# Index bits of the weight look-up: int32 and-operations on VectorE in place of float comparisons on GpSimd

## The chip, the cores and the metric

The kernel runs on one core of a Trainium2 chip. The core has a matrix engine (TensorE, PE in the rows), a vector engine (VectorE, DVE), an activation engine (ScalarE, ACT), a general engine (GpSimd, POOL) and an engine that issues transfers (SyncE, SP), all working side by side on a memory of 128 partitions (SBUF); matmuls write to PSUM. The metric is the device time of one execution in microseconds, the median of several.

## The reference, cut to what matters

Four layers, each an attention-like block and a feed-forward block, are applied to x (4 x 256 tokens of 256 values). The change touches the weights of the third feed-forward block, which come as 4-bit indices into a table of 16 numbers:

```python
def _ghost_linear(x, idx, lut):
    w = lut[idx]                       # lut: 16 floats, idx: int32 in 0..15
    return jnp.einsum('bsh,oh->bso', x, w)
gate = _ghost_linear(x, gate_idx, lut) # 688 x 256 indices
up = _ghost_linear(x, up_idx, lut)     # 688 x 256
h = jax.nn.silu(gate) * up
return _ghost_linear(h, down_idx, lut) # 256 x 688
```

The look-up itself needs only the indices and the table. The kernel therefore does it ahead, beside the block before: the third attention (16 heads, 4 batches, two softmaxes on one set of queries).

## The kernel before, in words

Each engine has one program, written out by hand, and they meet through semaphores; there is no planner. What stands next on an engine's program waits for what stands before it.

The 4288 index words of each partition lie in `w2` (the tensor `regD`) and are looked up in `LUT_PIECES` = 8 pieces of `LP` = 536 words. With the index written in bits b3 b2 b1 b0, a piece goes so:
- Bits. GpSimd casts the piece to float in `left` (`lut_b0`, two buffers, L611), and three times compares with 8, 4 or 2, times that number (the mask `lut_m`, L613), and subtracts (L614). What remains in `left` is b0 as 0.0 or 1.0. `lut_bits` counts pieces.
- Leaves. ScalarE computes, for each pair of table entries, `lut[2*leaf] + b0 * (lut[2*leaf+1] - lut[2*leaf])` over the piece (L979, `lut_leaves`): 8 leaves of a piece in 4 calls of 2 (`k` = 0 to 3).
- Picks. VectorE's `copy_predicated` chooses between leaves by the masks of 2, 4 and 8 (L1612, `choose` in `lut_step`): 7 picks, counted by `lut_pick`. The result replaces the indices in `w2`.

All of this is threaded through the attention's 64 steps (batch b, head h, i = 16 b + h). Piece p starts at VectorE's step i = `LUT_START` + `LUT_STEPS` * p = 5 + 7 p; its sub-steps 2 to 6 are the picks, and ScalarE has its leaves at sub-steps 1 to 4. GpSimd is not threaded: its loop over the pieces runs on its own, held back only by `lut_pick` of the piece two before, which frees the buffers (and by `q2_mm` for piece 1, whose masks lie in the room of `xnT`).

In a step of the attention, TensorE does the shifted scores of head h (L2218, L2219), some scores of the next batch (L2198), and the values of the head before (L2234); ScalarE takes the exponential (L994); VectorE takes the maxima of the next batch's scores (L1574, L1575), which free the score banks, and every fourth head normalises (L1593 to L1599). At h = 13 VectorE splits the next batch's maxima into three bf16 parts (L1582 to L1585); TensorE transposes them (L2205), ScalarE copies them out (L969), and the next batch's shifted scores need them. In between stand the query projection of the second half (L2066, L1402 and what follows), the splitting of queries (L963 to L1567), the output product (L2083) and its addition (L1420, L1421). The feed-forward block that uses the weights begins near 852 us.

Names of tensors in the rows: `regD` holds the pieces and one `left`, `regC` the other `left` and a leaf, `regB` the masks of even pieces and a leaf, `xnT` the masks of odd pieces, `ctxT` a leaf.

Of the kernel before, what the change touches and what calls it, by code (L numbers as in the profile page):

```python
# [17 lines left out]
I32 = mybir.dt.int32  # L18
U32 = mybir.dt.uint32
ALU = mybir.AluOpType  # L20
ACT = mybir.ActivationFunctionType
# [3 lines left out]
B, S, DIM, CDIM = 4, 256, 256, 128  # L25
# [37 lines left out]
def build(nc, a, out):  # L63
    with ExitStack() as ctx:
        def sb(name, shape, dt=F32):
            return ctx.enter_context(nc.sbuf_tensor(name, shape, dt))

        def sem(name):
            return ctx.enter_context(nc.semaphore(name))
# [31 lines left out]
        def carve(region):  # L101
            at = [0]

            def take(*shape, dt=F32):
# [9 lines left out]
                if len(shape) > 1:  # L114
# [138 lines left out]
        w2 = regD[:, 0:2 * NG + ND]  # L253
# [3 lines left out]
        LUT_PIECES = 2 * B  # L257
        LP = (2 * NG + ND) // LUT_PIECES
# [7 lines left out]
        lut_b0 = [w2_room, lut_b0]  # L266
        lut_m = [[tB(LP) for _ in range(3)], xnT_room]
        lut = sb("lut", [P, LUT])
        lutd = sb("lutd", [P, LUT // 2])
# [31 lines left out]
        ld_raw, ld_1, ld_f1, ld_2, ld_i2, ld_3, ld_f3 = (  # L301
            sem(n) for n in ("ld_raw", "ld_1", "ld_f1", "ld_2", "ld_i2", "ld_3", "ld_f3"))
# [9 lines left out]
        stk_f, stk_h, stk_r, stk_m, stk_done, stk_tr, stk_out, shift_set, v2_set = (  # L312
            sem(n) for n in ("stk_f", "stk_h", "stk_r", "stk_m", "stk_done", "stk_tr", "stk_out", "shift_set", "v2_set"))
        q2_mm, q2_out, s2_mm, max2, mxs_done, mx_tr, mxT_done, st_mm, exp2, o2_mm, o2_norm, co_tr, coT_done, wo2_mm, wo2_add = (
            sem(n) for n in ("q2_mm", "q2_out", "s2_mm", "max2", "mxs_done", "mx_tr", "mxT_done", "st_mm", "exp2", "o2_mm",
                             "o2_norm", "co_tr", "coT_done", "wo2_mm", "wo2_add"))
        lut_bits, lut_leaf, lut_pick, sx_done, z_done, z_tr, z_add, bf_done, hw_mm, wd3_done, hs3_done, xh_mm, xh_out = (
            sem(n) for n in ("lut_bits", "lut_leaf", "lut_pick", "sx_done", "z_done", "z_tr", "z_add", "bf_done", "hw_mm", "wd3_done",
                             "hs3_done", "xh_mm", "xh_out"))
        stored = sem("stored")  # L320

# [115 lines left out]
        def _(pool):  # L437
            chain = [0]

            def link(ins, base=0):  # L440

                chain[0] += 1
                ins.then_inc(plc, 1)
                pool.wait_ge(plc, base + chain[0])
# [76 lines left out]
            with pool.Fori(1, H0 // 2 - 1) as hp:  # L521
                for par in range(2):
                    n = hp * 2 + (par - 2)
# [76 lines left out]
                    pool.tensor_tensor(shiftw, shift0[:, 0:H2].unsqueeze(2).to_broadcast([STK, H2, S]),  # L600
                                       shift0[:, H2:].unsqueeze(1).to_broadcast([STK, H2, S]), ALU.mult).then_inc(shift_set, 1)

            pool.wait_ge(ld_i2, 16 * 5)
            pool.wait_ge(stk_out, 4 * B)
            for i in range(LUT_PIECES):
                left = lut_b0[i % 2]
                if i == 1:
                    pool.wait_ge(q2_mm, 4)
                if i >= 2:
                    pool.wait_ge(lut_pick, 7 * (i - 1))  # L610
                link(pool.tensor_copy(left, w2[:, i * LP:(i + 1) * LP].bitcast(I32)))  # L611
                for m, bit in zip(lut_m[i % 2][::-1], (8.0, 4.0, 2.0)):
                    link(pool.tensor_scalar(m, left, bit, bit, ALU.is_ge, ALU.mult))  # L613
                    ins = pool.tensor_tensor(left, left, m, ALU.subtract)  # L614
                    if bit > 2:
                        link(ins)
                ins.then_inc(lut_bits, 1)
            for n in range(10, 12):
                ln_pow(n)

# [1 line left out]
            for st in range(3):  # L622
                step = 1 << st
                src = bf[st % 2].rearrange("p (g two s) n -> p g two s n", two=2, s=step)
                dst = bf[(st + 1) % 2].rearrange("p (g two s) n -> p g two s n", two=2, s=step)
# [11 lines left out]
        def _(act):  # L637
# [186 lines left out]
            for b in range(B):  # L824
                act.wait_ge(nb1_done, b + 1)
                for q in range(2):
                    act.activation(p1[b][:, q, :], bank(b)[:, q * S:(q + 1) * S], ACT.Exp,
                                   bias=nb1[:, b, q:q + 1], accum_out=ls1[:, b, q:q + 1]).then_inc(exp1, 1)
# [15 lines left out]
            for tt in range(NT):  # L844
                for nb in range(2):
                    i = 2 * tt + nb
# [4 lines left out]
                if tt < B:  # L851
                    act.wait_ge(rl1_done, tt + 1)
                    for q in range(2):
                        last = act.activation(p1[tt][:, q, :], p1[tt][:, q, :], ACT.Copy, scale=ls1[:, tt, q:q + 1])
# [116 lines left out]
            def lut_leaves(i, k):  # L971

                act.wait_ge(lut_bits, i + 1)
                used = 7 * i + (0, 0, 1, 3)[k]
                if used:
                    act.wait_ge(lut_pick, used)
                to = (w2[:, i * LP:(i + 1) * LP], lutC, lutD, lutC)[k]
                for dst, leaf in ((to, 2 * k), (lut_alt[k % 2], 2 * k + 1)):
                    last = act.activation(dst, lut_b0[i % 2], ACT.Identity, scale=lutd[:, leaf:leaf + 1], bias=lut[:, 2 * leaf:2 * leaf + 1])  # L979
                last.then_inc(lut_leaf, 1)  # L980

            act.wait_ge(df_mm, 2 * TPH)
# [5 lines left out]
            for b in range(B):  # L988
                for h in range(H2):
                    i = b * H2 + h  # L990
                    act.wait_ge(st_mm, i + 1)
                    if i >= 3:
                        act.wait_ge(o2_mm, i - 2)
                    act.activation(pT2[i % 3].rearrange("p k q -> p (k q)"), bank(4 + i % 2), ACT.Exp,  # L994
                                   scale=float(HD2) ** -0.5).then_inc(exp2, 1)
                    if h in STACK2 and b + 1 < B:
                        stack_out(B + b + 1, STACK2.index(h))
                    if b == 0 and h == LNT9:
                        ln_out(9)
                    if b == 0 and h == QNORM + 2:  # L1000
                        deviations(B + 1, TPH)
                    if b + 2 < B and h == SPLIT2[b]:
                        stack_parts(b + 2)
                    if h == COT2 and b:
                        heads_out2(b - 1)
                    if h == SHIFT2 and b + 1 < B:
                        maxima_out(b + 1)
                    piece, step = divmod(i - LUT_START, LUT_STEPS)
                    if 0 <= piece < LUT_PIECES and 1 <= step < 5:
                        lut_leaves(piece, step - 1)  # L1010
# [8 lines left out]
        def _(dve):  # L1019
# [586 lines left out]
            def lut_step(i, step):  # L1606

                A = w2[:, i * LP:(i + 1) * LP]
                m1, m2, m3 = (m.bitcast(U32) for m in lut_m[i % 2])

                def choose(to, m, other):
                    dve.copy_predicated(to, m, other).then_inc(lut_pick, 1)  # L1612

                n = 7 * i
                if 2 <= step <= 5:
                    k = step - 2
                    if k == 0:
                        dve.wait_ge(lut_bits, i + 1)
                    dve.wait_ge(lut_leaf, 4 * i + k + 1)
                    choose((A, lutC, lutD, lutC)[k], m1, lut_alt[k % 2])  # L1620
                    if k % 2:
                        dve.wait_ge(lut_pick, n + (2, 5)[k // 2])
                        choose((A, lutD)[k // 2], m2, lutC)
                elif step == 6:
                    dve.wait_ge(lut_pick, n + 6)
                    choose(A, m3, lutD)

# [5 lines left out]
            for b in range(B):  # L1633
                for h in range(H2):
                    i = b * H2 + h
                    if b + 1 < B:
                        for hn in first_pass(b, h):
                            maxima(b + 1, hn)
                        if h == SHIFT2 - 1:
                            maxima_parts(b + 1)  # L1640
                    if b == 0 and h == LN9:
                        dve.wait_ge(df_add, TPH * 2)
                        layer_norm(9)
                    if b == 0 and 0 <= h - QNORM < 3:
                        queries(1, h - QNORM)
                    piece, step = divmod(i - LUT_START, LUT_STEPS)
                    if 0 <= piece < LUT_PIECES:
                        lut_step(piece, step)
                    if b + 2 < B and h == SPLIT2[b]:
                        stack_rest(b + 2)  # L1650
                    if h % HPB == 2 and i >= HPB:
                        normalise((i // HPB - 1) // HPB, (i // HPB - 1) % HPB)
                    if h == WO2 and b:
                        output2(b - 1)
                    if b == B - 1 and h == WO2 + 2:
                        dve.wait_ge(wo2_add, 2)
                        layer_norm(10)
# [719 lines left out]
```

## Time and profile before

| | us |
|---|---|
| median of 3 runs | 1029.34 (1029.27 to 1031.43) |
| the profiled execution | 1028.96 |
| its span, first to last instruction | 1027.4 |
| PE busy | 867.6 |
| DVE busy | 708.8 |
| ACT busy | 535.8 |
| POOL busy | 448.0 |
| mean granted clock of PE | 0.92 of full |

Times in the rows are microseconds from the span's start unless they are marked ns. A line such as L1612 is a line of the kernel's text. In "out<-in" the tensor written stands first, then those read, then partitions x elements and the type. "idle" is the time that the engine stood before an instruction, and the name behind the arrow is what ended it. An engine's idle time costs nothing unless the engine is on the path to the end, so the rows are to be read as a question: what is late at this point, and for whom.

### The profile page before, as it was taken

What the parts mean: (1) busy time and instruction counts of PE and PEld (TensorE: products, weight loads), DVE (VectorE), ACT (ScalarE), POOL (GpSimd) and SP (SyncE); (2) the same over time, 40 slices, a digit from 0 to 9 for tenths busy, and PEclk for the clock granted to TensorE, in tenths of its full rate; (3) what the DMA queues carried; (4) which work ended last, traced back from release to release, by engine and by line L of the source; (5) the groups of instructions that cost most, each with busy time, mean ns of one, the idle gap of its engine ahead of it and who ended that gap; (6) DMA issues with size and microseconds to landing.
All of it is one profiled execution on the core that took longest, in us unless ns stands there. A gap on an engine that the chain in (4) does not pass through costs nothing.

```text
span 1027.4 us, 13071 instructions
## 1 busy us (share of the span) xinstructions
PE 867.6 (84%) x4348; PEld 615.1 (60%) x4352; DVE 708.8 (69%) x1367; ACT 535.8 (52%) x991; POOL 448.0 (44%) x274
## 2 busy tenths in 40 slices
PE   5795899999999999645579986858688799999998
PEld 3354777777877777513354643728577685545646
DVE  4247689999899998778848566765989863353311
ACT  2486687787778778733313442535678472112120
POOL 1211678777778886556810002007458540600000
PEclk8898899999999999866879998958699899999999
DMA  4003000100000100000520000000000001100000
GB/s 126 16 5 133 16 17 16 31 15 15 15 15 15 31 3 6 1 0 1 198 83 0 1 1 1 1 0 1 2 1 2 1 1 48 83 0 1 12 9 21
DMA packets 12924, 24.25 MB, mean 24 GB/s; under 512 B 4280, under 2 KB 8656, under 8 KB 11728
## 3 DMA queue, kind: packets, MB, share of 16 engines
q1 hardware_dynamic: 12448, 20.53, 6.2%
q10 hardware_dynamic: 432, 3.15, 0.8%
q8 instruction: 26, 0.43, 0.2%
q14 instruction: 18, 0.15, 0.0%
HBM read 22.63 MB, written 1.05 MB: 23 GB/s over the span
## 4 chain that ended last, share of the span: by engine, by line
PE 30%; DVE 14%; issue 4%; ACT 4%; POOL 1%; ACTq 0%; DVEq 0%
PE PS L2131 12%; PE PS L2180 6%; PE PS L2234 3%; DVE mxf L1574 2%; DVE regD L1612 1%; PE PS L2035 1%; PE PS L1674 1%; DVE regB L1612 1%; PE PS L2011 1%; PE PS L2198 1%; PE PS L2049 1%; PE PS L2218 1%; PE PS L2219 1%; DVE xn L1051 1%; PE PS L2083 1%
## 5 line engine op out<-in xcount | busy, mean ns | idle before, releaser
L487 POOL TENSOR_TENSOR X<-X,xn 128x512 f32<-128x512 f32 x62 | 103.4, 1668 | 69.1 <-ACT xn L712 68.6
L454 POOL TENSOR_SCALAR veps<-mv 128x4 f32<-128x4 f32 x16 | 3.6, 228 | 265.9 <-DVE mv L1042 265.8
L1141 DVE TENSOR_TENSOR_SCAN regB<-regB 128x1024 f32<-128x1024 f32 x32 | 85.5, 2671 | 0.2
L1122 DVE TENSOR_SCALAR_CACHE_REDUCE regA<-PS,nrq 128x256 bf16<-128x256 f32 x128 | 56.0, 475 | 38.2 <-PE PS L1749 36.3
L731 ACT ACTIVATE regA<-PS,nb,rq 128x256 f32<-128x256 f32 x128 | 72.1, 576 | 11.7 <-DVE regA L1122 10.9
L2234 PE MATMUL PS<-regA 128*128 128x128 f32 x512 | 74.8, 293 | 3.4 <-ACT regA L994 3.3
L480 POOL TENSOR_TENSOR y<-y,regB 128x1024 f32<-128x1024 f32 x32 | 75.7, 2364 | 3.5 <-DVE regB L1152 3.4
L1771 PE MATMUL PS<-regA 128*128 128x256 f32 x256 | 67.0, 384 | 7.3 <-DVE qss L1109 7.2
L2234 PEld LDWEIGHTS PS<-regA 128*128 128x128 f32 x512 | 68.2, 206 | 7.1 <-ACT regA L994 6.1
L1749 PE MATMUL PS<-regA 128*128 128x256 f32 x256 | 67.1, 385 | 0.0
L1780 PE MATMUL PS<-regA 128*128 128x256 f32 x256 | 66.5, 383 | 0.0
L1722 PE MATMUL PS<-xnT,regA 128*128 128x512 f32 x128 | 60.3, 614 | 4.6 <-ACT regA L702 3.4
L2131 PE MATMUL PS<-xnT,regB 128*128 128x512 f32 x128 | 61.2, 628 | 1.3 <-ACT xnT L642 1.3
L2180 PE MATMUL PS<-regB 128*128 128x256 f32 x256 | 58.8, 388 | 3.6 <-DVE X L1551 3.5
L933 ACT ACTIVATE regB<-PS 128x512 f32<-128x512 f32 (+1 forms) x28 | 16.7, 596 | 84.2 <-PE PS L2131 84.0
L2131 PE MATMUL PS<-regA,regB 128*128 128x512 f32 x128 | 55.8, 594 | 1.4 <-ACT regA L923 1.4
L2180 PEld LDWEIGHTS PS<-regB 128*128 128x128 f32 x256 | 49.2, 194 | 12.6 <-DVE X L1551 4.3
L1771 PEld LDWEIGHTS PS<-regA 128*128 128x128 f32 x256 | 47.3, 192 | 14.2 <-DVE qss L1109 8.4
L1749 PEld LDWEIGHTS PS<-regA 128*128 128x128 f32 x256 | 46.0, 193 | 15.4 <-issue 10.1
L737 ACT COPY regA<-PS 128x512 f32<-128x512 f32 x64 | 38.1, 596 | 29.8 <-PE PS L1760 29.6
L1780 PEld LDWEIGHTS PS<-regA 128*128 128x128 f32 x256 | 49.2, 192 | 6.9
L712 ACT ACTIVATE xn<-PS,ls 128x256 f32<-128x256 f32 x124 | 52.8, 491 | 0.2 <-issue 0.2
(276 smaller groups left out, 2162.6 us busy)
## 6 DMA issues: line engine op xcount, KB each, us to landing
regA<-in_W SPq DMA_DIRECT2D x16, 384.0 KB, 3.0
regB<-in_wg SPq DMA_DIRECT2D x2, 1024.0 KB, 6.5
regB<-in_wu SPq DMA_DIRECT2D x2, 1024.0 KB, 8.5
X<-in_x SPq DMA_DIRECT2D x1, 1024.0 KB, 8.2
regC<-in_wg ACTq DMA_DIRECT2D x1, 1024.0 KB, 5.8
regC<-in_wu ACTq DMA_DIRECT2D x1, 1024.0 KB, 8.0
regC<-in_wd ACTq DMA_DIRECT2D x1, 1024.0 KB, 10.0
regB<-in_wd SPq DMA_DIRECT2D x1, 1024.0 KB, 9.9
```

Of the source, the lines that this page charges most:

```text
L480: pool.tensor_tensor(halves(y3, i), halves(y3, i), halves(prod, i), ALU.add).then_inc(y_done, 1)
L487: pool.tensor_tensor(xt, xt, part, ALU.add).then_inc(x0_add, 1)
L731: act.activation(p0[i][:, q, :], bank(S_BANK + i)[:, q * S:(q + 1) * S], ACT.Exp, bias=nb0[:, i, q:q + 1], scale=rq[par][:, 2 * b + q:2 * ...
L1122: ins = dve.tensor_scalar(spill[:, i, q, :], bank(S_BANK + i)[:, q * S:(q + 1) * S], nrq[par][:, t:t + 1], None, ALU.mult, ALU.min, accum_ ...
L1141: dve.tensor_tensor_scan(v(hs), v(dA), v(dBu), 0.0, ALU.mult, ALU.add).then_inc(scan_done, 1)
L1722: last = pe.matmul(to[:, i * HALF:(i + 1) * HALF], w0[par][:, c * P:(c + 1) * P], xnT[:, c, i * HALF:(i + 1) * HALF], start=c == 0, stop=c ...
L1749: last = pe.matmul(bank(S_BANK + b % 2)[:, q * S:(q + 1) * S], qT[par][:, (2 * b + q) * P:(2 * b + q + 1) * P], kT[par][:, b * S:(b + 1) * S],
L1771: last = pe.matmul(bank(O_BANK)[:, 0:S], ctxN[:, 2 * b + k, :], pT0[b % 2][:, k, :], start=k == 0, stop=k == 1)
L1780: last = pe.matmul(bank(W_BANK)[:, q * DIM:(q + 1) * DIM], oT0[b % 2][:, q * P:(q + 1) * P], wvo[par], start=True, stop=True)
L2131: last = pe.matmul(bank(to)[0:rows, :], w[:, k, c * P:c * P + rows], src[:, k, :], start=k == 0, stop=k == KD - 1)
L2180: last = pe.matmul(bank(6 + td % 2)[:, 0:DIM], hT[0:rows, c, t * P:(t + 1) * P], wd[0:rows, c, :], start=c == 0, stop=c == nch - 1)
L2234: last = pe.matmul(bank(6 + g % 2)[:, at:at + P], pT2[i % 3][:, k, q * P:(q + 1) * P], V2flat[:, v:v + P], start=k == 0, stop=k == 1)
```

## The change

VectorE takes over the bits. At sub-step 0 of a piece (steps 5, 12, 19, 26, 33, 40, 47 and 54) it does four bitwise-ands of the piece as int32: with 2, 4 and 8 for the masks (not zero means choose), and with 1 for b0, which stays an int32 0 or 1. ScalarE reads b0 as int32 and converts it by itself. The loop on GpSimd goes. The waits for the buffers move to VectorE, a new semaphore `lut_mask` counts the masks, and `lut_bits` now comes with the and by 1.

```diff
@@ gpsimd
-            pool.wait_ge(ld_i2, 16 * 5)
-            pool.wait_ge(stk_out, 4 * B)
-            for i in range(LUT_PIECES):
-                left = lut_b0[i % 2]
-                if i == 1:
-                    pool.wait_ge(q2_mm, 4)
-                if i >= 2:
-                    pool.wait_ge(lut_pick, 7 * (i - 1))
-                link(pool.tensor_copy(left, w2[:, i * LP:(i + 1) * LP].bitcast(I32)))
-                for m, bit in zip(lut_m[i % 2][::-1], (8.0, 4.0, 2.0)):
-                    link(pool.tensor_scalar(m, left, bit, bit, ALU.is_ge, ALU.mult))
-                    ins = pool.tensor_tensor(left, left, m, ALU.subtract)
-                    if bit > 2:
-                        link(ins)
-                ins.then_inc(lut_bits, 1)
@@ scalar, lut_leaves
-                    last = act.activation(dst, lut_b0[i % 2], ACT.Identity, scale=lutd[:, leaf:leaf + 1], bias=lut[:, 2 * leaf:2 * leaf + 1])
+                    last = act.activation(dst, lut_b0[i % 2].bitcast(I32), ACT.Identity, scale=lutd[:, leaf:leaf + 1], bias=lut[:, 2 * leaf:2 * leaf + 1])
@@ vector, lut_step
                 A = w2[:, i * LP:(i + 1) * LP]
+                if step == 0:
+                    if i == 1:
+                        dve.wait_ge(q2_mm, 4)
+                    if i >= 2:
+                        dve.wait_ge(lut_pick, 7 * (i - 1))
+                    for m, bit in zip(lut_m[i % 2], (2, 4, 8)):
+                        dve.tensor_scalar(m.bitcast(I32), A.bitcast(I32), bit, None, ALU.bitwise_and).then_inc(lut_mask, 1)
+                    dve.tensor_scalar(lut_b0[i % 2].bitcast(I32), A.bitcast(I32), 1, None, ALU.bitwise_and).then_inc(lut_bits, 1)
...
                     if k == 0:
-                        dve.wait_ge(lut_bits, i + 1)
+                        dve.wait_ge(lut_mask, 3 * i + 3)
```

## Rows read from the trace of the kernel before

**Rows 1.** The page, part 1: busy us, share of the span, instructions.

```profile
PE 867.6 (84%) x4348; PEld 615.1 (60%) x4352; DVE 708.8 (69%) x1367; ACT 535.8 (52%) x991; POOL 448.0 (44%) x274
```

**Rows 2.** Stretches: length, busy us of each engine, PE's granted clock, DMA.

```profile
695.00:742.00 47.00, 35.68 (x243) 30.72 (x241) 34.77 (x70) 25.41 (x35) 27.70 (x19) 0.77 0.00 1
742.00:778.00 36.00, 30.55 (x271) 27.03 (x270) 31.27 (x72) 28.58 (x43) 23.09 (x15) 1.00 0.01 2
778.00:818.00 40.00, 32.24 (x270) 28.56 (x270) 35.19 (x72) 27.06 (x42) 27.77 (x18) 0.96 0.01 2
818.00:852.00 34.00, 31.16 (x243) 27.98 (x243) 25.05 (x55) 22.82 (x38) 12.30 (x9) 0.95 0.00 1
```

**Rows 3.** Chain that ended last, in order of time: start, us, what.

```profile
718.30 1.75 DVE regD L1612
...
739.79 0.88 DVE mxs L1582
...
778.55 1.89 DVE regD L1612
...
808.96 1.61 DVE regD L1612
```

**Rows 4.** Groups of POOL by shape: busy us, mean ns, idle before, releaser.

```profile
L613 POOL TENSOR_SCALAR xnT<-regC 128x536 f32<-128x536 f32 x12 | 26.0, 2168 | 1.1
...
L611 POOL CAST regC<-regD 128x536 f32<-128x536 int32 x4 | 2.5, 629 | 17.0 <-DVE regD L1612 11.8 <-PE PS L2066 5.2
...
L454 POOL TENSOR_SCALAR veps<-mv 128x4 f32<-128x4 f32 x1 | 0.2, 233 | 13.0 <-DVE mv L1042 13.0
```

**Rows 5.** Line 1612: ns min/median/max, first to last start; then its stretch.

```profile
L1612 DVE COPY_PREDICATED regB<-regB,regC x8: 742/758/1805, 723.2 to 832.4; 128x536 f32<-128x536 uint32 x8
...
L1612 DVE COPY_PREDICATED regD<-regB,ctxT x4: 750/752/755, 735.3 to 834.0; 128x536 f32<-128x536 uint32 x4
...
695.00:852.00 157.00, 54.06 (x56) 0.91 0.00 1
```

**Rows 6.** Lines 1574 and 1582: ns min/median/max.

```profile
L1574 DVE TENSOR_REDUCE mxf<-PS x64: 633/652/661, 678.9 to 815.8; 128x2 f32<-128x480 f32 x64
...
L1582 DVE CAST mxs<-mxf x4: 175/402/870, 691.0 to 817.1; 128x64 bf16<-128x64 f32 x4
```

**Rows 7.** Bitwise-ands in the trace, and DVE's timeline at 771 us.

```profile
L1197 DVE TENSOR_SCALAR regA<-regC x6: 672/673/674, 148.4 to 369.5; 128x1024 int32 x6
...
L1192 DVE TENSOR_SCALAR mx_am<-mx_am x6: 181/181/181, 128.0 to 349.0; 128x32 int32<-128x32 int32 x6
...
770.87 0.75 DVE L1612 COPY_PREDICATED regD<-regB,ctxT 128x536 f32<-128x536 uint32 x1
771.52 0.64 DVE L1574 TENSOR_REDUCE mxf<-PS 128x2 f32<-128x480 f32 x1
```

**Rows 8.** DVE's timeline: start, us, instruction, idle before it.

```profile
712.90 0.66 DVE L1574 TENSOR_REDUCE mxf<-PS 128x2 f32<-128x480 f32 x1 [2.79 <-PE PS L2198]
...
788.59 0.66 DVE L1574 TENSOR_REDUCE mxf<-PS 128x2 f32<-128x480 f32 x1 [1.72 <-PE PS L2198]
...
804.47 0.69 DVE L1420 TENSOR_TENSOR X<-X,regC 128x512 f32<-128x512 f32 x1 [1.59 <-PE PS L2083]
...
824.96 0.88 DVE L1612 COPY_PREDICATED regD<-regB,regC 128x536 f32<-128x536 uint32 x1 [3.72 <-ACT regC L979]
```

**Rows 9.** ACT's timeline.

```profile
738.58 0.83 ACT L979 ACTIVATE regD<-regC,lut,lutd 128x536 f32<-128x536 f32 x1
...
742.18 0.37 ACT L969 COPY regB<-PS 96x256 bf16<-96x256 bf16 x1 [1.57 <-PE PS L2205]
...
753.44 0.82 ACT L979 ACTIVATE regD<-regD,lut,lutd 128x536 f32<-128x536 f32 x1
```

**Rows 10.** PE's timeline: the output product twice.

```profile
801.28 3.15 PE L2083 MATMUL PS<-regC,regB 128*128 128x256 f32 x8
...
835.98 1.89 PE L2083 MATMUL PS<-regC,regB 128*128 128x256 f32 x8
```

More of the change, by code:

```diff
@@ L316, in build @@
                              "o2_norm", "co_tr", "coT_done", "wo2_mm", "wo2_add"))
-        lut_bits, lut_leaf, lut_pick, sx_done, z_done, z_tr, z_add, bf_done, hw_mm, wd3_done, hs3_done, xh_mm, xh_out = (
-            sem(n) for n in ("lut_bits", "lut_leaf", "lut_pick", "sx_done", "z_done", "z_tr", "z_add", "bf_done", "hw_mm", "wd3_done",
+        lut_bits, lut_mask, lut_leaf, lut_pick, sx_done, z_done, z_tr, z_add, bf_done, hw_mm, wd3_done, hs3_done, xh_mm, xh_out = (
+            sem(n) for n in ("lut_bits", "lut_mask", "lut_leaf", "lut_pick", "sx_done", "z_done", "z_tr", "z_add", "bf_done", "hw_mm", "wd3_done",
                              "hs3_done", "xh_mm", "xh_out"))
```

## The prediction

> **What bounds the kernel now.** I read the engines' shares first [rows 1]: PE is busy 84% of the span, VectorE (DVE) 69%, GpSimd (POOL) 44%. A mean over stages decides nothing, so next the busy time by stretch around the edited code [rows 2]. The look-up runs beside the 64 steps of the third attention, from 695 to 852 us, and each of the four stretches is about one of its batches. DVE is busy 34.8 of 47 us, then 31.3 of 36, then 35.2 of 40; only in the last batch does it fall to 25.1 of 34, while PE rises to 31.2. So DVE is the fullest engine in the second and third batch, with ScalarE (ACT) close in the second (28.6 of 36). Granted clock is 0.77 in the first stretch and about 1 in the others. The chain of waits says the same [rows 3]: picks (copy_predicated, L1612) and casts of DVE stand on it one after another.
>
> **What is removed.** POOL makes the bits of each piece in one cast (L611), three comparisons (L613) and three subtractions (L614). Per piece that is 0.63 + 3 x 2.16 + 3 x 1.34 = 11.1 us, in all 2.9 + 2.5 + 26.0 + 25.9 + 16.3 + 15.8 = 89.4 us of POOL's 448 ([rows 4] have one line of each buffer). None of it is itself on the path: the last piece's bits were done at 831.9 and its leaves start at 835.3, and the gap is as wide or wider at the others. POOL's next work, the power of a layer norm at 844.88, waited 13.0 us for DVE [rows 4], so it comes no earlier by an empty POOL. Directly the removal is worth 0.
>
> Indirectly it is worth something. A pick takes 742 to 755 ns at its shortest, but up to 1.9 us elsewhere with the same shape; the 56 of them take 54.06 us where 56 x 0.755 = 42.3 would do [rows 5]. Each long one starts or runs while a POOL instruction of a piece is under way; those of 838 us and later, after POOL's last piece, are all 0.76 to 0.77. Casts of 128x64 show it too (870 against 175 ns) and so does one addition by 1.0 us, while the maxima, which read PSUM, stay within 633 to 661 ns [rows 6]. Excess: picks 11.8, casts and remainder-casts 1.7, the addition 1.0, together 14.4 us. By batch it is 2.0, 2.9, 6.9 and 2.6.
>
> The Trainium skill (SBUF — State Buffer, section "SBUF: two separate sides") states that VectorE and GpSimd share one port pair as an exclusive lock, taken for a whole instruction by a VectorE instruction with two SBUF inputs or in a two-port mode, the loser standing still. The trace agrees: picks read two SBUF tensors and stretch by up to 1.1 us, PSUM maxima do not. By that rule the whole 14.4 us goes with POOL's pieces; without it a part could belong to ACT's traffic. It also says that the new operations would stand behind POOL if POOL still ran, which it does not.
>
> **What is added.** 4 bitwise-ands per piece, 32 in all, 128x536 int32. No such shape is in the trace, but its neighbours are: the same operation on 128x1024 takes 673 ns, on 128x32 181 ns [rows 7]. Between them 181 + 504 x 492/992 = 431 ns. Bounds: 181 below; above, 673. I take 0.43, 13.8 us of busy time. On DVE's timeline an instruction without a wait starts 0.10 us before the last one ends (a pick of 0.75 us at 770.87, the next maximum at 771.52 [rows 7]), so four ands push what follows by about 4 x 0.35 = 1.4 us (0.7 to 2.7 with the bounds). No real wait comes with them: q2_mm 4 was already waited for at step 7, the lut_pick counts are DVE's own and a piece old. DVE's total is then 32 x 0.35 = 11.2 us more against 14.4 less. ACT's leaves now read int32 in place of float. No row of ACT has such an input; on DVE the int32 form differs from a float one of the same size by 22 ns (673 to 695), which on 64 leaves is at most 1.4 us either way, half of it where ACT is full. I take 0.
>
> **Where the 1.4 us lands.** The ands stand at steps 5, 12, 19, 26, 33, 40, 47, 54 of DVE's program, and ACT's leaves one step later wait for the last of the four. By pieces:
> - Piece 0 (near 707): DVE then waits 2.79 us before 712.90 [rows 8]. Free.
> - Piece 1 (step 12, behind the maxima ending 739.8): on the chain, +1.4. Ahead of it the pick at 718.30 gives back 1.0, behind it the two casts 1.0 [rows 3]. That leaves -0.6, but ACT, which began its leaves at 738.58, now stands until about 740.2, and the shift copy L969 behind them (742.18) comes no earlier [rows 9]. Sum 0.
> - Piece 2 (step 19, 752.8): DVE 1.0 late at once, ACT's leaves 0.8 late against 753.44 [rows 9]. Picks at 755.6, 758.3 and 759.6 give back 1.2 and DVE's short waits 0.5. At 761.5: -0.5.
> - Piece 3 (step 26, 772.2): DVE has no gap there, +1.4; the cast at 776.5 gives back 0.4, the pick at 778.55 (1.88 us, ACT waits for it) 1.1 [rows 3]. At 780: -0.6.
> - Piece 4 (step 33, 785.8): DVE waits 1.72 us before 788.59 [rows 8]. Free. Then the picks at 789.3, 792.8 and 797.1 give back 2.4 us, but the leaves that they read come from an ACT whose timeline has no gap over 0.35 us from 783 to 796, so I count 1.4 of it. At 801: -2.0.
> - Piece 5 (step 40, 802.8): DVE waits 1.59 us for the output product before 804.47 [rows 8]. Free. Picks at 808.87 and 812.79, both on the chain, the first among the rows [rows 3], give back 0.95 + 0.87. At 818: -3.8.
> - Piece 6 (step 47, 821.2): 3.72 us of waiting before 824.96 [rows 8]. Free. The pick at 826.82 gives back 1.0, of which ACT can use the 0.58 us it waited: -4.4.
> - Piece 7 (step 54, 834.7): DVE has by then 2.5 us more in hand from three shorter picks, ACT's leaves at 835.3 do not wait. Free. From 852 on nothing differs.
>
> Sum -4.4 us. The profiled execution took 1028.96 us, 1027.4 of it span and 1.6 around it; it lies 0.4 under the median of 1029.34. So 1024.6 for a profile like this one and 1024.9 for the median; I say 1025.
>
> **The rivals.** What a measurement here can tell from no change is about 0.2%, 2.1 us.
> - The gain is eaten by ACT and PE. The attention's steps go round DVE, ACT and PE, and ACT is full from 742 to 761 and from 783 to 796. If ACT's pace holds there and again past 806, only the 0.6 of piece 3 and 1 us or so of the 806 to 818 stretch remain: about 1028. For it: ACT 28.6 of 36 us [rows 2]. Against: its waits for DVE's picks in the third batch.
> - Slower. The ands sit in front of ACT's leaves and of the maxima that PE's next scores wait for; at pieces 1, 2 and 3 there is no gap, 3 x 1.4 = 4.2 us, and PE idle there can bring its clock down. The clock's price: the output product of 8 matmuls took 3.15 us at 801.28 after an idle 2 us against 1.89 at 835.98 [rows 10]. With 1.3 to 2.6 for one or two such stretches and a give-back of only 3, it is +3: 1032. It decides if the four ands take more than about 0.5 us a step each, for then piece 4 and 5 outgrow their gaps as well.
> - More than forecast. With DVE ahead, PE does not idle at 799 to 801 and 816 to 818, and the clock stays up: 1.3 (above) and 1 us for the steps at 819 to 822 more. And ACT's caps at 797 fall: 1021.5.
> - The change does not free DVE: the picks stay long without POOL. Then 11.2 us of ands have nothing against them, about half on the path: 1034. The late picks of 0.76 us speak against it, and so does the port rule named above; I give it little.
>
> **How the numbers follow.** Forecast (own range 1022.5 to 1027) 0.52; eaten 0.19; more 0.15; slower by the leaves' wait 0.10; picks stay long 0.04. Faster by over 0.2% (under 1027.3) is the forecast, the larger gain and a sliver of the eaten case: 0.69. Within: most of the eaten case and the mild part of the slower: 0.19. Slower: 0.12. The range takes the larger gain and the eaten case whole and the unknown cost of the ands to its middle: 1020.5 to 1030.5.
>
> **What would show it.** Right: POOL almost empty between 696 and 844; 56 picks at about 42 us, none above 0.8 us; casts near 0.2 us; ands at 0.43 us and 0.35 apart, 13.8 us in all; ACT waiting about 1.6 us for the bits of piece 1 and 0.5 to 1 at pieces 2 and 3, none at 4 to 7; the batches ending 0, 0.6, 3.8 and 4.4 us earlier than 742, 778, 818 and 850. Wrong: ands at 0.6 us or more; picks still of 1 us and over; ACT waiting for bits in the third batch; a clock under 0.9 between 742 and 818; or leaves of over 0.85 us from int32 input.

## The result, and the profile after

The changed kernel takes 1024.55 us (median of 4 runs, 1023.6 to 1025.03) beside 1029.39 for the kernel before: ratio 0.9939 [0.9927, 0.9950]. A second set of runs gave 1024.51 beside 1029.89, 0.9945 [0.9933, 0.9958]. The medians lie 4.8 and 5.4 us apart, and by the ratios it is faster by 6.3 and 5.7 us; 1025.0 was forecast. The profiled execution of after took 1025.03 us, 1023.5 of it span.

The page of the kernel after, part 1, answers to [rows 1]: VectorE is 4.5 us less busy, GpSimd 88.

```profile
PE 867.3 (85%) x4352; PEld 613.2 (60%) x4352; DVE 704.3 (69%) x1399; ACT 535.3 (52%) x991; POOL 360.0 (35%) x218
```

The stretches of [rows 2], after (length, then PE, PEld, DVE, ACT and POOL, granted clock, DMA share, GB/s). Compare the third: PE is busy 36.4 of 40 us where it was 32.2, and the clock is 1.00 in it and in the fourth, where it was 0.96 and 0.95. (The edges of the stretches are fixed, and this execution came to the third attention 2.3 us later than that of before, so a row does not hold quite the same work in both.)

```profile
695.00:742.00 47.00, 36.18 (x252) 31.46 (x252) 34.17 (x78) 25.76 (x35) 1.26 (x2) 0.82 0.00 1
742.00:778.00 36.00, 28.00 (x244) 24.53 (x244) 30.00 (x77) 28.07 (x42) 0.00 (x0) 1.00 0.01 1
778.00:818.00 40.00, 36.41 (x320) 32.53 (x321) 36.55 (x94) 30.23 (x48) 0.00 (x0) 1.00 0.01 2
818.00:852.00 34.00, 30.77 (x234) 26.18 (x232) 22.86 (x59) 23.32 (x37) 1.26 (x2) 1.00 0.00 1
```

DVE's groups by shape in 690 to 850 us of after (busy us, mean ns, idle before). The ands (L1600, L1601) take 431 to 435 ns in the mean of each group, 32 x 0.432 = 13.8 us (the busy column counts their overlaps once). The casts whose median was 402 ns [rows 6] have one of 184.

```profile
L1600 DVE TENSOR_SCALAR xnT<-regD 128x536 int32<-128x536 int32 x12 | 4.5, 433 | 0.0
L1600 DVE TENSOR_SCALAR regB<-regD 128x536 int32<-128x536 int32 x12 | 4.5, 431 | 0.0
...
L1601 DVE TENSOR_SCALAR regC<-regD 128x536 int32<-128x536 int32 x4 | 1.7, 435 | 0.0
L1601 DVE TENSOR_SCALAR regD<-regD 128x536 int32<-128x536 int32 x4 | 1.7, 432 | 0.0
```

The picks, now L1605 (min/median/max ns, first to last start). All 56 lie between 742 and 780 ns; before, the first of these forms went up to 1805 [rows 5].

```profile
L1605 DVE COPY_PREDICATED regB<-regB,regC x8: 742/759/770, 724.6 to 827.4; 128x536 f32<-128x536 uint32 x8
...
L1605 DVE COPY_PREDICATED regD<-regB x4: 754/770/780, 725.3 to 824.3; 128x536 f32<-128x536 uint32 x4
```

The leaves, now L964, from int32 input: as long as from float before ([rows 9] show 0.82 and 0.83).

```profile
L964 ACT ACTIVATE regC<-regD,lut,lutd x16: 817/823/842, 711.4 to 826.5; 128x536 f32<-128x536 int32 x16
```

The chain of waits of after, in order of time (start, us, what). Ands stand on it at pieces 1, 2, 3 and 5, 1.04 + 0.35 us each time, and at no other.

```profile
741.06 1.04 DVE xnT L1600 x3
742.10 0.35 DVE regC L1601
...
755.05 1.04 DVE regB L1600 x3
756.09 0.35 DVE regD L1601
...
774.18 1.04 DVE xnT L1600 x3
775.22 0.35 DVE regC L1601
...
803.38 1.04 DVE xnT L1600 x3
804.42 0.35 DVE regC L1601
```

ACT's timeline in after, the leaves that waited for bits. It stands 2.16 us at piece 1, 0.70 and 0.90 at pieces 2 and 3, and 0.91 at piece 6, where none was expected; 0.25 at piece 0.

```profile
742.49 0.83 ACT L964 ACTIVATE regD<-regC,lut,lutd 128x536 f32<-128x536 int32 x1 [2.16 <-DVE regC L1601]
...
756.47 0.83 ACT L964 ACTIVATE regD<-regD,lut,lutd 128x536 f32<-128x536 int32 x1 [0.70 <-DVE regD L1601]
...
775.60 0.83 ACT L964 ACTIVATE regD<-regC,lut,lutd 128x536 f32<-128x536 int32 x1 [0.90 <-DVE regC L1601]
...
820.01 0.83 ACT L964 ACTIVATE regD<-regD,lut,lutd 128x536 f32<-128x536 int32 x1 [0.91 <-DVE regD L1601]
```

**Where the time went, batch by batch.** One profiled execution enters the third attention earlier or later than another for reasons ahead of it (691.0 to 694.6 us among these traces). So every kernel is measured from its own first cast of the maxima (the mxs cast, L1582 before, L1567 after) to the same cast of each later batch and to the last normalising product. These lengths repeat to 0.1 us between the two traces of the changed kernel. In this table, worked out from DVE's timelines, each column is one batch.

| us | batch 0 | 1 | 2 | 3 | sum |
|---|---|---|---|---|---|
| before | 48.8 | 36.7 | 40.6 | 34.6 | 160.6 |
| after | 49.0 | 37.4 | 34.6 | 33.2 | 154.3 |
| e1, POOL works beside it | 51.3 | 42.9 | 37.7 | 35.1 | 167.0 |
| e2, no ands at pieces 2 to 7 | 49.0 | 35.5 | 34.3 | 32.2 | 151.0 |
| e5, 7 ands a piece | 50.0 | 39.7 | 37.8 | 35.0 | 162.6 |
| e3, pieces 1 to 3 on POOL | 48.8 | 36.7 | 34.6 | 33.2 | 153.2 |
| e4, ands a step earlier | 49.1 | 37.7 | 34.6 | 32.2 | 153.6 |
| e8, pieces 0 and 1 ahead | 47.7 | 36.8 | 35.8 | 33.2 | 153.6 |
| e7, before with matmuls | 48.8 | 36.7 | 39.5 | 32.6 | 157.5 |
| e7 again | 48.8 | 36.7 | 38.3 | 34.6 | 158.3 |
| e10, after with matmuls | 49.0 | 37.4 | 34.6 | 33.2 | 154.2 |
| e9, ahead and POOL | 47.7 | 36.7 | 34.6 | 33.2 | 152.3 |
| e11, that and a step earlier | 47.7 | 36.7 | 34.6 | 32.2 | 151.2 |

The change loses 1.0 us in batches 0 and 1 and gains 6.0 in batch 2 and 1.3 in batch 3: 6.3 in all. What comes before and behind the stage decides how much of that one execution shows. Behind it the traces of before, after and a0_after take 175.8 to 175.9 us each; but after entered the stage 2.3 us later than before did and a0_after 0.9 later, so their profiled executions are only 3.9 and 5.4 us shorter. The stage is the measure of the change, and the total carries this variation with it.

### The profile page after: what moved, and what is told of

It is laid out like the page before. It is cut to its first block, busy times and chain, and to the rows that moved or that the text cites. A ratio compares the mean times of both kernels' runs of the same rounds, so it can differ in the third digit from the quotient of the medians.

```text
span 1023.5 us, 13050 instructions
## 1 busy us (share of the span) xinstructions
PE 867.3 (85%) x4352; PEld 613.2 (60%) x4352; DVE 704.3 (69%) x1399; ACT 535.3 (52%) x991; POOL 360.0 (35%) x218
## 3 DMA queue, kind: packets, MB, share of 16 engines
q10 hardware_dynamic: 432, 3.15, 0.8%
HBM read 22.63 MB, written 1.05 MB: 23 GB/s over the span
## 4 chain that ended last, share of the span: by engine, by line
PE 30%; DVE 13%; ACT 5%; issue 4%; POOL 1%; ACTq 0%; DVEq 0%
PE PS L2124 12%; PE PS L2173 6%; PE PS L2227 3%; DVE mxf L1559 2%; PE PS L2028 1%; PE PS L1667 1%; PE PS L2004 1%; PE PS L2042 1%; ACT regC L964 1%; PE PS L2191 1%; DVE xn L1036 1%; PE PS L2211 1%; PE PS L2212 1%; ACT regA L979 1%; PE PS L1944 1%
## 5 line engine op out<-in xcount | busy, mean ns | idle before, releaser
L454 POOL TENSOR_SCALAR veps<-mv 128x4 f32<-128x4 f32 x16 | 3.6, 227 | 396.3 <-DVE mv L1027 396.2
L1107 DVE TENSOR_SCALAR_CACHE_REDUCE regA<-PS,nrq 128x256 bf16<-128x256 f32 x128 | 56.0, 475 | 37.6 <-PE PS L1742 35.8
L2227 PEld LDWEIGHTS PS<-regA 128*128 128x128 f32 x512 | 65.8, 200 | 6.9 <-ACT regA L979 5.7
L1764 PEld LDWEIGHTS PS<-regA 128*128 128x128 f32 x256 | 47.3, 192 | 14.2 <-DVE qss L1094 8.4
L1742 PEld LDWEIGHTS PS<-regA 128*128 128x128 f32 x256 | 45.4, 190 | 14.5 <-issue 9.6
L1773 PEld LDWEIGHTS PS<-regA 128*128 128x128 f32 x256 | 49.2, 192 | 6.9
```

What stands on the lines that cost most here:

```text
L1107: ins = dve.tensor_scalar(spill[:, i, q, :], bank(S_BANK + i)[:, q * S:(q + 1) * S], nrq[par][:, t:t + 1], None, ALU.mult, ALU.min, accum_ ...
L1742: last = pe.matmul(bank(S_BANK + b % 2)[:, q * S:(q + 1) * S], qT[par][:, (2 * b + q) * P:(2 * b + q + 1) * P], kT[par][:, b * S:(b + 1) * S],
L1764: last = pe.matmul(bank(O_BANK)[:, 0:S], ctxN[:, 2 * b + k, :], pT0[b % 2][:, k, :], start=k == 0, stop=k == 1)
L1773: last = pe.matmul(bank(W_BANK)[:, q * DIM:(q + 1) * DIM], oT0[b % 2][:, q * P:(q + 1) * P], wvo[par], start=True, stop=True)
L2227: last = pe.matmul(bank(6 + g % 2)[:, at:at + P], pT2[i % 3][:, k, q * P:(q + 1) * P], V2flat[:, v:v + P], start=k == 0, stop=k == 1)
```

## Experiments: does GpSimd's silence free VectorE?

The theory: picks and casts were long because GpSimd's pieces ran beside them. The rival: something else in the stage made them long, and the new order of work happened to shorten them. The unchanged kernel after was run along with the first four as their yardstick (a0_after).

> The changed kernel again, as the yardstick on this chip. All theories: 1024.5 us (1023.6 to 1025.0), 56 picks of 128x536 at 42.5 us in all, 32 ands at 0.43 us.

Measured 1024.51 us; picks 42.5 us in all, ands 423 to 434 ns.

**e1_pool_copy** puts the old loop back on GpSimd, on spare memory, so that VectorE makes the bits that are used.

```diff
+            for i in range(LUT_PIECES):
+                left = spare_b
...
+                link(pool.tensor_copy(left, y3[:, :, :, :].rearrange("p c b l -> p (c b l)")[:, 0:LP].bitcast(I32)))
+                for bit in (8.0, 4.0, 2.0):
+                    link(pool.tensor_scalar(spare_m, left, bit, bit, ALU.is_ge, ALU.mult))
+                    link(pool.tensor_tensor(left, left, spare_m, ALU.subtract))
```

> The changed kernel, with GpSimd's old loop of 56 instructions running again on memory that nobody else uses, held by the same waits as before; its results are not used. Theory L (the gain is VectorE time that GpSimd's instructions had taken by holding a port): the picks stretch again to about 54 us in all with single ones of 1.9 us, the ands stretch too (to 0.6 us and more on average), and the time goes above that of the kernel before: the old stretch of 14 us back plus ands, 1029.4 + 3 to 6 = 1032 to 1036. Rival M (the gain comes from the masks being made in VectorE's own order, so that nothing waits for GpSimd; the long picks were chance or ACT's traffic): stays at 1024.5, picks at 42 us.

Measured 1037.49 us, ratio to before 1.0070 [1.0058, 1.0082]: 13.0 above the changed kernel, and above the 1032 to 1036 that were expected. Its trace by line, first an and, then a pick of the same form as above:

```profile
L1615 DVE TENSOR_SCALAR xnT<-regD x12: 420/466/1231, 742.2 to 843.9; 128x536 int32<-128x536 int32 x12
```

```profile
L1620 DVE COPY_PREDICATED regB<-regB,regC x8: 740/754/1729, 725.8 to 841.0; 128x536 f32<-128x536 uint32 x8
```

Both are long again, and their shortest ones are unchanged. The 56 picks take 49.2 us against 42.5, less than the 54 that were expected; the 32 ands take 0.58 us in the mean. That it is a wait and not slower work, the timeline of before shows: the 11 stretched picks that met a subtraction of GpSimd (L614) all end 0.61 to 0.63 us after it does, whenever they started. The six stretched ones that met only a comparison (L613) all end 0.75 to 0.76 us before the comparison's recorded end. One of each (start, us):

```profile
744.28 2.56 POOL L613 TENSOR_SCALAR regB<-regD 128x536 f32<-128x536 f32 x1
...
745.05 1.04 DVE L1612 COPY_PREDICATED regD<-xnT,regB 128x536 f32<-128x536 uint32 x1
...
782.35 1.33 POOL L614 TENSOR_TENSOR regD<-regD,regB 128x536 f32<-128x536 f32 x1
782.41 1.88 DVE L1612 COPY_PREDICATED regB<-xnT,regC 128x536 f32<-128x536 uint32 x1
```

In e1 the four ands that started during a cast or a subtraction of GpSimd end 0.29 us after it. PE's clock suffers too, and this is a part that the expectation left out. The two middle stretches of e1:

```profile
742.00:778.00 36.00, 26.76 (x216) 23.74 (x214) 29.88 (x64) 25.52 (x37) 19.50 (x12) 0.91 0.01 1
778.00:818.00 40.00, 33.85 (x276) 29.99 (x277) 37.90 (x84) 26.93 (x42) 27.44 (x18) 0.91 0.00 1
```

The rival falls. The Trainium skill (SBUF — State Buffer, section "SBUF: two separate sides") has VectorE and GpSimd share one port pair as an exclusive lock; the trace agrees, as far as picks from SBUF stretch to 1.7 us and more while the PSUM maxima did not [rows 6], and as far as a pick stands until GpSimd's subtraction has ended. It does not agree that the lock is always held for the whole instruction: the pick at 745.05 ended 0.75 us before the comparison that it met, though the recorded ends of GpSimd's instructions are rough. The section names for VectorE's side two SBUF inputs and the two-port modes, which tensor_scalar can enter. The ands are a tensor_scalar with one SBUF input, and they stretch to 1231 ns; that they run in such a mode is not shown otherwise.

## Experiments: what do the ands cost, and where?

**e2_few_ands** leaves the ands out from piece 2 on; leaves and picks run on old bits, so the values looked up for pieces 2 to 7 are not those of the reference.

```diff
-                if step == 0:
+                if step == 0 and i < 2:
```

> The changed kernel without the ands of pieces 2 to 7; those pieces reuse the bits of pieces 0 and 1 (their looked-up values are left out). Prices the ands. By the trace of the changed kernel the ands of pieces 1, 2, 3 and 5 stand on the chain of waits with 1.4 us each; three of these are taken away here, and ACT's waits for them. Theory L: 3 x 1.4 = 4.2 us less, 1020.3 (1019.5 to 1022). Rival H (the ands are hidden, the stage is paced by ACT and PE): within 1 us of 1024.5.

Measured 1020.66 us, 0.9904 [0.9890, 0.9917]: 3.9 below the changed kernel where 4.2 was expected, 3.2 of it in the stage. The sum came out, its parts (pieces 2, 3 and 5 at 1.4 each) did not. The table tells where: batch 1 is 1.9 us shorter without pieces 2 and 3, batch 2 only 0.3 without 4 and 5, batch 3 1.0 without 6 and 7. So a place on the chain (piece 5) is no price: when its 1.4 us went, something else was nearly as late.

**e5_more_ands** adds three ands into spare memory at each piece.

```diff
+                    for extra in spare:
+                        dve.tensor_scalar(extra.bitcast(I32), A.bitcast(I32), 2, None, ALU.bitwise_and)
```

> The changed kernel with three more ands per piece, ahead of the four, into memory that nobody reads: 24 x 0.43 us busy, 24 x 0.35 = 8.4 us of VectorE's time, 1.05 per piece. Theory L (VectorE's time is what counts on the stretches without a gap): pieces 1, 2, 3 and 5 pay in full, 4.2 us, others nothing: 1028.7 (1027.5 to 1030.5), about the kernel before. Rival H: under 1 us, 1025.5. If all eight paid it were 1033.

Measured 1031.33 us, 1.0012 [1.0003, 1.0021]: 6.8 above the changed kernel where 4.2 was expected, and above the stated 1030.5. The stage grew by 8.35 us, which is all of the ands' 24 x 0.35 = 8.4, though the changed kernel's own 32 cost only some 4.5 of their 11.2 (3.2 by e2, 1.3 by e8). The third stretch of e5 shows what came on top of the ands themselves, a granted clock of 0.91 where after has 1.00:

```profile
778.00:818.00 40.00, 35.51 (x286) 31.26 (x287) 35.58 (x92) 29.16 (x46) 0.00 (x0) 0.91 0.00 1
```

In it PE's value groups of eight matmuls at 780.27 and 782.83 take 1.91 us, where 1.06 is usual. So with three ands more a piece the change would have gained nothing: the mechanism of the rival "slower" is there, its point was not reached.

**e4_early** issues the same four ands one step earlier, so that ACT finds the bits ready.

```diff
+        EARLY = -1
...
-                if step == 0:
+                if step == EARLY:
```

> The changed kernel with the ands of each piece one step of the attention earlier. ACT stands 5.0 us in all before its leaves for the ands (L1600, L1601) in the changed kernel; here it should not stand at all. Theory L says that VectorE's time is what counts and ACT's stand is hidden behind it: 1024.3, within 0.7 of the changed kernel. Rival W (the wait for the bits has taken the place of the stretch, and costs what is left): 1.5 to 3 us less, 1022.

(This set and the last had the kernel before at 1030.91 us, 1.0 above the first; differences to the changed kernel are between medians, and by the ratios they would be about 1 us larger.)

Measured 1023.73 us, 0.9929 [0.9915, 0.9942]: 0.8 below the changed kernel, within what the runs can tell from nothing. The stage is 0.7 shorter, and the table puts it in batch 3 (-1.0) and not at piece 1, where ACT had stood longest: batches 0 and 1 are even 0.1 and 0.2 longer, although ACT waits for bits only once in its trace, 0.24 us at piece 3. So ACT's waits at pieces 1 to 3 had no price of their own, VectorE's 1.4 us had; the 0.91 us at piece 6 was on the path.

**e3_mixed** gives GpSimd pieces 1, 2 and 3 back and leaves 0 and 4 to 7 on VectorE.

```diff
+        ON_POOL = (1, 2, 3)
...
-                if step == 0:
+                if step == 0 and i not in ON_POOL:
```

> The changed kernel, but pieces 1, 2 and 3 get their bits from GpSimd in the old way; pieces 0 and 4 to 7 by ands on VectorE. Theory L by the stretch of each piece: the pieces on GpSimd cost the chain 1.0 (pick at 718) + 1.0 (casts at 740) + 0.8 (picks at 758 to 760), 2.8 us in the old trace, the ands of the same three pieces 3 x 1.4 = 4.2 us: 1.4 less than the changed kernel, 1023.1 (1022 to 1024.5). Rival M (it matters that VectorE makes its bits itself): above 1025.5.

Measured 1022.69 us, 0.9911 [0.9895, 0.9926]: 1.8 below the changed kernel. The stage is 1.0 shorter (the profiled execution was the slowest of the five, 1026.85 us: it entered the stage 2.7 us later than a0_after's and took 1.6 more behind it). Its batches 0 and 1 are before's to 0.05 us and its batches 2 and 3 are after's. The two halves of the change thus do not lean on each other: ands are dearer than GpSimd's disturbance up to piece 3, cheaper from piece 4 on.

**e8_two_first** makes the bits of pieces 0 and 1 before the attention loop, where DVE waits (spare memory for the masks of piece 1).

```diff
+            dve.wait_ge(stk_tr, 4 * B)
+            for i in range(2):
+                lut_ands(i)
             stack_rest(1)
```

> The changed kernel with the ands of pieces 0 and 1 moved ahead of the attention's loop, into the 6.8 us in which VectorE waits for ACT at 670 us (piece 1's masks go to memory of their own). Takes 1.4 us of ands off the chain at 741 us, and ACT's longest wait for bits (2.2 us). Theory L: 1.4 to 2 us less than the changed kernel, 1022.8. Rival H (hidden): 1024.5.

Measured 1022.50 us, 0.9922 [0.9908, 0.9936]. Batch 0 is 1.3 us shorter and batch 1 0.6: the ands of piece 1 did cost nearly their full 1.4. Batch 2 gave 1.2 of it back in this profile, and that is PE's clock: at 774.28 and 776.42 its value groups of eight matmuls take 1.49 and 1.89 us where 1.05 and 1.06 are usual, together 1.3 more. The granted clock of 742 to 778 us is 0.95 in e8 and 1.00 in a0_after. In e9 and e11, which also have pieces 0 and 1 ahead, it stayed up; what made it fall in e8 is open.

## Experiments: how much is the clock?

PE's clock in the third batch was another difference between the traces, so it was taken by itself: **e7_clock** is the kernel before with 24 small matmuls of no use at two places where PE idled in that batch (ahead of the output product and at the batch's end).

```diff
+            def keep_busy(n):
+                for _ in range(n):
+                    pe.matmul(bank(0)[:, 0:P], identb[:, :], identb[:, :], start=True, stop=True)
...
+                        if b == 2 and h == 7:
+                            keep_busy(24)
...
+                                if b == 2:
+                                    keep_busy(24)
```

> The kernel before, with 24 small matmuls of no use put in front of TensorE's wait for the maxima at step 39, and 24 in front of the one at the end of the third batch (801 and 818 us). Tests whether TensorE's lower clock there was a cost of its own: the output product took 3.15 us after the idle stretch against 1.89 elsewhere, and the steps at 818 to 822 ran at the lower clock. Theory C (part of the gain is the clock): 1.3 + 1.0 = 2.3 us less than before, minus what the added matmuls delay, 1027.5 to 1028.5 where before is 1029.9. Rival L alone (VectorE's time only): no change or slower, 1029.9 to 1031.

Measured 1026.96 us, 0.9954 [0.9939, 0.9969]; in a later set

> The kernel before with the two groups of matmuls, once more, on the same chip as the changed kernel with them. 1026.5 to 1027.5 by the first run.

1025.26 us, 0.9943 [0.9929, 0.9957]. It is faster than the kernel before by 4 to 6 us with more work and nothing taken away, both times by more than was expected: 3.1 and 2.3 us of it in the stage, 2.1 each time behind it (below). In PE's timeline of e7 (start, us, what) the added group stands at 800.16, and the output product behind it takes 1.89 us where it took 3.15 [rows 10]; but the value group at 814.99 still takes 1.68.

```profile
800.16 1.51 PE L2240 MATMUL PS<-identb 128*128 128x128 bf16 x24
...
804.49 1.89 PE L2083 MATMUL PS<-regC,regB 128*128 128x256 f32 x8
...
814.99 1.68 PE L2234 MATMUL PS<-regA 128*128 128x128 f32 x8
```

The same place in PE's timeline of the changed kernel (a0_after), with no matmul added: PE waits 1.25 us where it waited 1.99 in before, and the product takes 1.89.

```profile
800.10 0.38 PE L2191 MATMUL PS<-regA,regB 96*128 96x256 bf16 x2 [1.25 <-DVE mxf L1560]
800.32 1.89 PE L2076 MATMUL PS<-regC,regB 128*128 128x256 f32 x8
```

Short windows of PE in three kernels (length, PE busy, granted clock, DMA). First before, then a0_after, then e7_clock:

```profile
795.00:803.00 8.00, 5.57 (x38) 0.92 0.00 0
803.00:812.00 9.00, 8.26 (x62) 0.88 0.00 0
812.00:825.00 13.00, 10.28 (x76) 0.87 0.01 3
```

```profile
795.00:803.00 8.00, 6.57 (x49) 1.00 0.00 0
803.00:812.00 9.00, 8.42 (x74) 1.00 0.01 3
812.00:825.00 13.00, 10.14 (x86) 1.00 0.00 1
```

```profile
795.00:803.00 8.00, 6.76 (x72) 1.00 0.01 2
803.00:812.00 9.00, 8.16 (x67) 1.00 0.00 0
812.00:825.00 13.00, 11.40 (x100) 0.87 0.01 3
```

**e10_after_clock** adds the same matmuls to the kernel after. If the clock was already up there, they can win nothing in the stage.

> The changed kernel with the same two groups of 24 small matmuls as the last experiment on the clock. In the changed kernel TensorE keeps its full clock in the third batch without them, so they can only delay. Theory C+L (of the change's gain about half is VectorE's time, half the clock that stays up by it): 1 to 2 us slower than the changed kernel, 1025.5 (1024.5 to 1026.5), so that only some 2 us are left between it and the kernel before with the same matmuls. Rival L (VectorE's time only): the matmuls cost both kernels alike, 5 us are left between the two, 1022.

In the stage they win nothing: 154.21 us against 154.24 and 154.28. So of the change's 6.3 us there, some 2.3 to 3.1 is the clock, which is what the matmuls won in the kernel before (158.3 and 157.5 against 160.6), and 3.3 to 4.1 is left for VectorE's time. The clock's part may be larger, because e7's clock still fell to 0.87 after 812 us; or smaller by up to 0.6, because the stretch of VectorE in batches 2 and 3 was 9.3 and 9.5 us in the two runs against 10.0 in before. The rows of before and a0_after put it at 3.0 us: the output product 3.15 against 1.89, the value group behind it (804.22 and 802.05) 1.51 against 1.05, and two value groups after the batch's end (818.26, 820.41 and 814.13, 815.51) 1.50 and 1.91 against 1.11 and 1.06.

The total missed its expectation all the same: 1021.64 us, 0.9908 [0.9894, 0.9922], 2.9 below the changed kernel. 2.1 of that come from a place that neither the change nor the matmuls touch, 60 us later; the rest is within the spread of the runs. Windows of a0_after and then of e10 there:

```profile
852.00:880.00 28.00, 26.04 (x75) 13.73 (x74) 10.07 (x21) 2.98 (x5) 7.00 (x11) 0.96 0.33 119
880.00:900.00 20.00, 20.00 (x60) 10.55 (x60) 7.28 (x23) 2.86 (x5) 10.77 (x8) 0.97 0.01 1
```

```profile
852.00:880.00 28.00, 27.66 (x87) 14.65 (x86) 8.95 (x23) 2.98 (x5) 5.10 (x8) 1.00 0.32 120
880.00:900.00 20.00, 19.07 (x55) 9.41 (x54) 7.93 (x25) 3.35 (x6) 12.54 (x11) 1.00 0.00 0
```

and the group of PE that stands at the seam, once in each:

```profile
877.61 4.74 PE L2173 MATMUL PS<-regD,regB 128*128 128x256 f32 x12 [1.96 <-DVE X L1536]
```

```profile
876.63 3.05 PE L2173 MATMUL PS<-regD,regB 128*128 128x256 f32 x12 [0.34 <-DVE X L1536]
```

From one layer norm's power on GpSimd (L454, at 872.84 in a0_after) to the next it takes 20.1 to 20.2 us in before, after, a0_after, e2, e4, e8 and e11, 18.0 in both traces of e7 and in e10, 18.5 in e5 and e9, 21.8 in e1 and e3. So some 2 us are in play there in every version and are not the change's. Two things are at work there, and both are known from the stage before it. The first is GpSimd beside VectorE. Their timelines in a0_after, then in e10:

```profile
874.16 0.72 POOL L612 TENSOR_TENSOR regA<-regA 128x256 f32<-128x256 f32 x1
874.22 3.00 DVE L1036 TENSOR_SCALAR xn<-X,mv,rstd 128x256 f32<-128x256 f32 x4 [1.47 <-POOL rstd L455]
```

```profile
874.86 1.38 DVE L1036 TENSOR_SCALAR xn<-X,mv,rstd 128x256 f32<-128x256 f32 x4 [1.47 <-POOL rstd L455]
...
876.17 0.72 POOL L612 TENSOR_TENSOR regA<-regA 128x256 f32<-128x256 f32 x1 [1.34 <-DMA regB<-in_wu]
```

In a0_after GpSimd's sums and differences run beside VectorE's four normalisations, which take 0.81 us each; in e10 GpSimd waits for a load of weights until they are done, and they take 0.41. That is the difference between the two waits of PE, 1.6 us. GpSimd waits so in e10 and both traces of e7 and in no other. The second is PE's clock behind the long wait: with that wait it fell in most programs (852 to 900 us: 0.96 and 0.97 in a0_after, 1.00 and 0.83 in e3), but not in e5 and e9 (1.00 and 1.00). Why the load came later just in the three programs with added matmuls stays open.

## Experiments: a version that beats both

**e9_two_first_mixed** puts the parts together that won: pieces 0 and 1 ahead of the loop, 2 and 3 on GpSimd, 4 to 7 by ands.

> Ands of pieces 0 and 1 ahead of the loop, pieces 2 and 3 on GpSimd in the old way, 4 to 7 by ands on VectorE. Theory L adds the two savings of the separate experiments as far as they are of different pieces: 1.4 to 2 for piece 1, and for pieces 2 and 3 the ands' 2.8 against a stretch of 1.8, 1.0: 1021.5 where the changed kernel has 1024.5. If the stretch by GpSimd brings the clock down somewhere, 1023.5.

1020.97 us, 0.9905 [0.9889, 0.9921]. **e11_best** adds to it the ands of 4 to 7 one step earlier.

> As the one before, and the ands of pieces 4 to 7 one step earlier, so that ACT never waits for them. Theory L: 0.3 us less than that, 1021.2; the step at which piece 5's ands stand is full either way. If it gains 1 us or more, ACT's waits were on the path.

1021.11 us, 0.9898 [0.9882, 0.9914]. Both beat the changed kernel by 3.4 us or more; between them the runs see no difference, though e11's stage is 1.1 us shorter. Behind the stage e9 takes 174.2 us and e11 175.7, by the clock in the place of the last section: 1.7 us of e9's gain lie there and not in the stage, of e11's only 0.1.

## Why the prediction was right, by its own steps

- **The removal is worth 0 directly.** Nothing speaks against it. GpSimd's next power waits for VectorE as before. (In passing, "the gap is as wide or wider at the others" was wrong for piece 0, whose bits were done at 706.2 with leaves at 707.96; it changed no number.)
- **The stretch of 14.4 us goes.** Right: picks at 42.5 us, none above 0.78, casts at 0.185, and e1 brings stretch back. The rival by which picks stay long is out.
- **An and takes 0.43 us, four push 1.4.** Right to 5 ns; leaves from int32 cost nothing, as taken.
- **Where the 1.4 lands.** Near in the sum (3.8 us of cost forecast, 4.5 measured), off in the parts. Piece 1 cost 1.3 (e8, forecast 1.4) and pieces 2 and 3 1.9 together (e2, forecast 1.0 and 1.4). Piece 5 was said to be free behind VectorE's wait for the output product; in the changed kernel that wait is gone, the ands stand on the chain, and yet they cost little: 4 and 5 together 0.3. Pieces 6 and 7 were said to be free and cost 1.0, by way of ACT's wait (below).
- **What is given back.** Right up to 801 us. Take marks that both traces have and count each from the kernel's own entry (a0_after less before): the shift copy of 742.18 comes 0.1 us earlier (forecast 0), ACT's exponential of 781.99 0.4 (forecast 0.6 at 780), the maximum of 800.17 1.9 (forecast 2.0 at 801). The table's columns of batches 0 and 1 seem to say otherwise, +0.2 and then +1.0 us in all. But they end where the casts begin, ahead of the 1.0 and the 0.4 + 1.1 us that the prediction books behind these points; its own sum there is +0.4 and +0.9. Behind 801 the output product and the value group took 1.7 us less, for which the sum had no term: the exponential of 806.21 comes 3.5 us earlier, and the cast of 817.08 5.0 where 3.8 was forecast.
- **ACT's waits.** 2.2, 0.7 and 0.9 us at pieces 1 to 3 where 1.6 and 0.5 to 1 were said, and free of cost by e4. "None at 4 to 7" failed at piece 6: 0.9 us, which is the 1.0 above.
- **The end of the stage.** -4.4 us was forecast, -6.3 came. VectorE's time is some 3.3 to 4.1 of it, so the sum was a little too large for what it counted. Piece 6 shows where: its 0.6 us came (0.7 between the exponentials of 826.69 and 831.26), but just ahead of it ACT's wait for the ands had taken 1.0, for which the sum had nothing. The term that it lacked is a clock that stays up after 800 and 816 us. It had been priced at 1.3 + 1 in the rival "more than forecast" and is worth 2.3 to 3.1. That rival happened in part: its mechanism is shown, its 1021.5 was not reached.
- **How much of the closeness is luck.** Two errors of opposite sign left the stage 1.9 us, nearly a third of its gain, off the forecast. The medians, 4.8 and 5.4 us apart, hide most of that. In the profiled executions it is what lies ahead of the stage that hides it, for after entered the stage 2.3 us later than before did; that the medians differ for the same reason is likely and not shown. The mechanism was right and the clock's term missing; that the total came within 0.5 us of 1025.0 is luck.
- **Eaten by ACT and PE.** Out for batches 2 and 3. **Slower.** Out, but e5 shows that three more ands a piece (2.4 us in place of 1.4) would have gone even.

## What to carry to other kernels

Where VectorE and GpSimd work side by side on SBUF, count the stretch of VectorE's instructions (their sum less the count times the shortest) and set it against what the moved work costs on VectorE; here 14.4 us stood against 11.2, piece by piece with another sign. Then look for what the engine behind it gains: less idle time of PE was worth about as much as VectorE's own time, because its clock stayed at the upper level. Move parts, not the whole: the versions that chose the engine piece by piece came to 0.990 where the whole change gave 0.994, and their stages were 2.0 and 3.0 us shorter than the changed kernel's. And measure such a change from a common point in the two traces, since the total also moves with places that it does not touch, here by 2 us and more.

## What the runs showed of the hardware

- An int32 bitwise-and with a constant, 128x536 in SBUF, takes 0.43 us on VectorE; GpSimd's comparison of the same shape took 2.16 [rows 4].
- ScalarE's activation costs the same from int32 as from float: 0.82 us for 128x536.
- A pick of VectorE that meets a subtraction of GpSimd ends 0.61 to 0.63 us after it (11 picks of before), one that meets a comparison 0.75 us before the comparison's recorded end.
- One-input int32 ands of VectorE also stretch beside GpSimd, up to 1231 ns from 430 (e1).
- 48 useless matmuls of 128x128 bf16, 3 us of PE's work in its idle time, made the kernel before 3.1 and 2.3 us faster in the stage. The value group of eight took 1.06 us at the upper level of the granted clock and 1.5 to 1.9 after it had fallen, which it did behind waits of 1.99 and 2.08 us in before and not behind those of 1.25 and 1.22 us in a0_after; but it also fell behind one of 1.31 us in the second run of e7, so the length of the last wait alone does not tell.
